# Pixel loads issued by ScalarE, a head norm in smaller operations, and five shared-expert blocks inside the attention's tail

## What is computed

```python
h = patches(x) @ W.T + b                       # 768 pixels a patch
# differential attention, 16 heads of 2 x 8, causal, 49 tokens
q, k, v = split(layernorm(h) @ w_attn)
att = softmax(mask(q @ k.T / 8))               # two maps a head
out = (att[0] - lam * att[1]) @ v
out = out * rsqrt(mean(out**2, 16 numbers) + 1e-5) * gamma * 0.8
h = h + out @ w_proj
# mixture of experts: 16 experts of 128, top 2, and a shared one of 512
xt = layernorm(h)
w, inds = top2(softmax(xt @ Wg.T)); w = w / sum(w)
y = sum_k w[k] * We_down[inds[k]] @ (silu(We_gate[..] @ xt) * (We_up[..] @ xt))
s = (silu(xt @ Ws_gate.T) * (xt @ Ws_up.T)) @ Ws_down.T
h = h + y + sigmoid(xt @ Wsg.T) * s
```

## Time and profile before

| | us |
|---|---|
| median of 3 runs (lowest, highest) | 452.35 (452.29, 455.34) |
| profiled execution | 452.69 |
| its span | 450.8 |
| PE busy | 365.3 (81%) |
| POOL busy | 274.9 (61%) |
| DVE busy | 262.5 (58%) |
| ACT busy | 205.9 (46%) |

### The profile page before, as it was taken

One profiled execution on the slowest core, in us unless ns is written; L12 is line 12 of the kernel. 1 busy time (PEld: TensorE's weight loads), 2 busy tenths in 40 slices (PEclk: granted clock), 3 DMA queues, 4 the chain that ended last, 5 costly groups with the idle time before them and its releaser, 6 DMA issues.

```text
span 450.8 us, 10482 instructions
## 1 busy us (share of the span) xinstructions
PE 365.3 (81%) x3418; PEld 329.9 (73%) x3419; DVE 262.5 (58%) x662; ACT 205.9 (46%) x512; POOL 274.9 (61%) x384
## 2 busy tenths in 40 slices
...
GB/s 271 105 69 68 94 94 117 62 63 107 93 86 91 114 104 78 85 114 86 126 112 1 1 1 1 0 399 239 69 71 74 120 125 135 129 127 103 22 203 225
DMA packets 33344, 47.17 MB, mean 105 GB/s; under 512 B 4538, under 2 KB 26750, under 8 KB 32528
## 3 DMA queue, kind: packets, MB, share of 16 engines
...
...
## 4 chain that ended last, share of the span: by engine, by line
POOL 36%; PE 31%; issue 19%; DVE 8%; DMA 3%; SPq 2%; POOLq 1%; ACT 0%; DVEq 0%
PE bank L1067 16%; POOL rr L549 10%; PE pair L1067 5%; POOL on L526 4%; POOL x_l L495 4%; PE bank L1295 3%; POOL att L534 3%; POOL parts L508 3%; POOL sq L542 2%; PE bank L1259 2%; POOL wsh_l L592 2%; POOL hn2T_l L565 2%; POOL rs L503 2%; DMA xr<-xt 2%; DVE h L1057 2%
## 5 line engine op out<-in xcount | busy, mean ns | idle before, releaser
L1157 PE MATMUL pair<-vx,PT 113*113 113x128 f32 x512 | 69.5, 279 | 1.6 <-issue 1.6
L900 DVE TENSOR_REDUCE smax<-bank 128x8 f32<-128x392 f32 x64 | 36.1, 564 | 48.9 <-PE bank L1136 48.7
L1157 PEld LDWEIGHTS pair<-vx,PT 113*113 113x113 f32 x512 | 61.6, 180 | 2.8 <-issue 1.8
L631 POOL DMA_INDIRECT picked<-by,bid x40 | 39.5, 988 | 28.0 <-DVE by L1046 18.2
L723 ACT ACTIVATE PT<-bank 113x456 f32<-113x456 f32 x64 | 35.3, 552 | 41.1 <-PE bank L1146 40.1
L1146 PE MATMUL bank<-cs,Sm 114*113 114x114 f32 x256 | 41.9, 286 | 11.5 <-DVE Sm L908 11.5
L549 POOL TENSOR_TENSOR rr<-ms,half_neg 128x16 f32<-128x16 f32 x16 | 46.7, 2916 | 1.3
L1079 PE MATMUL bank<-wt_h,x_h 128*98 128x256 f32 x96 | 31.9, 333 | 17.8 <-POOL x_l L495 11.2
L611 POOL DMA_INDIRECT slots_x<-hn2x,slot_u x32 | 34.9, 1092 | 18.4 <-issue 9.1
L526 POOL TENSOR_TENSOR on<-raw,rz 128x256 f32<-128x256 f32 x32 | 20.1, 629 | 42.2 <-DVE rz L943 42.2
L495 POOL TENSOR_TENSOR x_l<-xr,x_h 128x588 fp32r<-128x588 f32 x16 | 24.9, 1556 | 31.5 <-ACT x_h L643 31.5
...
## 6 DMA issues: line engine op xcount, KB each, us to landing
...
```

Source lines behind the costliest of these rows:

```text
L631: G.indirect_dma_start(out=picked, out_offset=bass.IndirectOffsetOnAxis(ap=bid[q][:], axis=0), in_=by[q][:], in_offset=None, bounds_check= ...
L900: V.tensor_reduce(smax[u % 2][:], score_of(u), AX.X, ALU.max).then_inc(maxed, 1)
L1157: last = T.matmul(bank[4 + b][0:JT, m * 2 * VN:(m + 1) * 2 * VN].rearrange("p (j n) -> p j n", j=2), PT[b][:, m, 0:JT], vx[i % NVX][:, :, ...
```

## The change

It has these parts. SP issues only pixel loads 0 and 1; ACT issues the other 14, each in front of the split of the tile before it, once POOL has split the tile that last used the buffer. SP's stack copies follow each other without loads between them. The bias is loaded third and has a semaphore of its own, so that the first embedding doesn't wait for the small loads. In the embedding steps DVE makes `rest` before it normalises. The head norm becomes: DVE ms2, ACT Ln and Exp (a first inverse root r0), and four 128x16 operations on POOL (one Newton step, with the factor in the projection's weights changed to match). The exponentials of the routing weights go from ACT to POOL as powers of e, and what DVE makes of them stands behind the offsets. Shared-expert blocks 0 to 4 have all their products in slots 66 to 79 and their Silu, multiply and splits in slots 70 to 81 and in the routing; the multiplies of blocks 4 and 5 and their splits stand between routing operations. Expert weight splits begin with block 7, one a block.

```diff
-            for i in range(2, 10):
-                load_x(i)
-            for d in range(4 * PARTS):
-                if d % 4 == 0:
-                    load_x(10 + d // 4)
-                stack(0, d)
-            for g in range(1, NGRP):
+            for g in range(NGRP):
...
             def head_norm(t):
-                pool.wait_ge(ms_done, t + 1)
-                G.tensor_tensor(ms2[:], ms[:], eps_sq[:], ALU.add).then_inc(ms2_done, 1)
-                pool.wait_ge(ms2_done, t + 1)
+
+                pool.wait_ge(r0_done, t + 1)
+                G.tensor_tensor(nt1[:], r0[:], r0[:], ALU.mult).then_inc(newton, 1)
+                pool.wait_ge(newton, 4 * t + 1)
+                G.tensor_tensor(nt2[:], nt1[:], ms2[:], ALU.mult).then_inc(newton, 1)
+                pool.wait_ge(newton, 4 * t + 2)
+                G.tensor_tensor(nt3[:], three[:], nt2[:], ALU.subtract).then_inc(newton, 1)
+                pool.wait_ge(newton, 4 * t + 3)
                 need(pool, ao_done, t)
-                G.tensor_tensor(rr[:], ms2[:], half_neg[:], ALU.pow).then_inc(rr_done, 1)
-                pool.wait_ge(rr_done, t + 1)
+                G.tensor_tensor(rr[:], r0[:], nt3[:], ALU.mult).then_inc(newton, 1)
+                pool.wait_ge(newton, 4 * t + 4)
                 need(pool, ao_turned, t)
...
+            pool.wait_ge(gate_diff, 1)
+            pool.wait_ge(logit_done, NT)
+            G.tensor_tensor(ed[:], euler[:], dl[:], ALU.pow).then_inc(e_exp, 1)
+            G.tensor_tensor(ez[:], inverse_euler[:], logits[:, :, E], ALU.pow).then_inc(e_exp, 1)
...
+            def load_x(i):
+                act.wait_ge(x_lo, i - 1)
+                act.wait_ge(x_hi, i - 1)
+                act.dma_start(xr[i % 2][:].rearrange("p k t -> p (k t)"), xt[i * 128:(i + 1) * 128, :]).then_inc(x_in[i % 2], 16)
...
+                if i + 2 < NT:
+                    load_x(i + 2)
...
+            def shared_silu(v):
+                act.wait_ge(sh_g, v + 1)
+                need(act, sh_h, v)
+                A.activation(sgl[:], bank[2 * v % 4][:, 0:SH], ACT.Silu).then_inc(sh_silu, 1)
+
+            def shared_high(v):
+
+                act.wait_ge(sh_h, v + 1)
+                need(act, sh_y, 4 * (v // SB - 1))
+                A.activation(hs_h[v // SB % 2][:, v % SB, :], hs[:], ACT.Copy).then_inc(sh_hi, 1)
+
+            SILU_AT = {70: 0, 72: 1, 73: 2, 76: 3, 81: 4}
+            HIGH_AT = {72: 0, 73: 1, 75: 2, 77: 3}
...
+                if (t := tile_at(u, 9)) is not None:
+                    act.wait_ge(ms2_done, t + 1)
+                    A.activation(lnr[:], ms2[:], ACT.Ln).then_inc(ln_done, 1)
+                    act.wait_ge(ln_done, t + 1)
+                    need(act, newton, 4 * t)
+                    A.activation(r0[:], lnr[:], ACT.Exp, scale=-0.5).then_inc(r0_done, 1)
...
+                if u in HIGH_AT:
+                    shared_high(HIGH_AT[u])
+                if u in SILU_AT:
+                    shared_silu(SILU_AT[u])
...
-            act.wait_ge(gate_diff, 1)
-            A.activation(ed[:], dl[:], ACT.Exp).then_inc(e_exp, 1)
-            A.activation(ez[:], logits[:, :, E], ACT.Exp, scale=-1.0).then_inc(e_exp, 1)
...
+            for v in range(DRAINED - 1, NU):
+                if v >= DRAINED:
+                    shared_silu(v)
+                shared_high(v)
+                if 0 <= v - FIRST_SPLIT < NG:
+                    split_expert(v - FIRST_SPLIT)
...
-                if 0 <= i - 1 < NT:
-                    norm(i - 1)
                 if i - 1 in QK_STEP:
                     n = QK_STEP[i - 1]
                     qk_rest(n, bank[n % 2])
+                if 0 <= i - 1 < NT:
+                    norm(i - 1)
...
+            def shared_hidden(v):
+                dve.wait_ge(sh_silu, v + 1)
+                dve.wait_ge(sh_u, v + 1)
+                need(dve, sh_hi, v)
+                need(dve, sh_lo, v)
+                V.tensor_tensor(hs[:], sgl[:], bank[(2 * v + 1) % 4][:, 0:SH], ALU.mult).then_inc(sh_h, 1)
+
+            def shared_low(v):
+                dve.wait_ge(sh_hi, v + 1)
+                need(dve, sh_y, 4 * (v // SB - 1))
+                V.tensor_tensor(hs_l[v // SB % 2][:, v % SB, :], hs[:], hs_h[v // SB % 2][:, v % SB, :].bitcast(F32), ALU.subtract).then_inc(sh_lo, 1)
+
+            HIDDEN_AT = {71: 0, 73: 1, 74: 2, 76: 3}
+            LOW_AT = {72: 0, 74: 1, 75: 2, 77: 3}
...
+                    dve.wait_ge(ms_done, t + 1)
+                    need(dve, newton, 4 * t - 2)
+                    V.tensor_scalar(ms2[:], ms[:], 1.0 / 16.0, EPS, ALU.mult, ALU.add).then_inc(ms2_done, 1)
+                if u in LOW_AT:
+                    shared_low(LOW_AT[u])
+                if u in HIDDEN_AT:
+                    shared_hidden(HIDDEN_AT[u])
...
-            dve.wait_ge(e_exp, 2)
-            link(V.tensor_scalar(ed1[:], ed[:], 1.0, None, ALU.add))
-            link(V.reciprocal(w1[:], ed1[:]))
-            V.tensor_tensor(w2[:], w1[:], ed[:], ALU.mult).then_inc(weights_known, 1)
-            link(V.tensor_scalar(ez1[:], ez[:], 1.0, None, ALU.add))
-            V.reciprocal(sig[:], ez1[:]).then_inc(weights_known, 1)
+            shared_hidden(DRAINED - 1)
...
+            shared_low(DRAINED - 1)
...
+            shared_hidden(DRAINED)
...
+            shared_low(DRAINED)
...
+            dve.wait_ge(e_exp, 2)
+            link(V.tensor_scalar(ed1[:], ed[:], 1.0, None, ALU.add))
+            link(V.reciprocal(w1[:], ed1[:]))
+            V.tensor_tensor(w2[:], w1[:], ed[:], ALU.mult).then_inc(weights_known, 1)
+            link(V.tensor_scalar(ez1[:], ez[:], 1.0, None, ALU.add))
+            V.reciprocal(sig[:], ez1[:]).then_inc(weights_known, 1)
+
+            shared_hidden(DRAINED + 1)
+            shared_low(DRAINED + 1)
...
+            for v in range(DRAINED, NU + DOWN_LAG):
+                if DRAINED + 2 <= v < NU:
+                    shared_hidden(v)
+                    shared_low(v)
+                if 0 <= v - FIRST_SPLIT < NG:
+                    split_expert(v - FIRST_SPLIT)
+                shared_down(v - DOWN_LAG)
...
-            SHARED_AT = {66: (0, 0), 67: (0, 1), 69: (1, 0), 70: (1, 1)}
+            SHARED_AT = {66: (0, 0), 67: (0, 1), 69: (1, 0), 70: (1, 1), 71: (2, 0), 72: (2, 1), 73: (3, 0), 75: (3, 1), 76: (4, 0), 79: (4, 1)}
...
+            for v in range(DRAINED, NU + DOWN_LAG):
+                if v < NU:
+                    shared_product(v, 0)
+                    shared_product(v, 1)
+                shared_down(v - DOWN_LAG)
```

More of the change, by code:

```diff
@@ L1 @@
+import math
 from contextlib import ExitStack
@@ L138, in build @@
         up_bf = keep("up_bf", [128, 128], BF16)
+        euler = keep("euler", [TT, NT])
+        inverse_euler = keep("inverse_euler", [TT, NT])
         shared = Zone(kept.at, ceiling)
@@ L185, in build @@
         pad = ea("pad", [128, ROW])
-        half_neg = ea("half_neg", [128, 2 * HP])
-        eps_sq = ea("eps_sq", [128, 2 * HP])
+        half_neg = ea("half_neg", [128, 1])
+        three = ea("three", [128, 2 * HP])
         eps_1 = ea("eps_1", [128, 1])
@@ L213, in build @@
         ms2 = ea("ms2", [128, 2 * HP])
+        lnr = ea("lnr", [128, 2 * HP])
+        r0 = ea("r0", [128, 2 * HP])
+        nt1 = ea("nt1", [128, 2 * HP])
+        nt2 = ea("nt2", [128, 2 * HP])
+        nt3 = ea("nt3", [128, 2 * HP])
         rr = ea("rr", [128, 2 * HP])
@@ L222, in build @@
         la = late.take
-        we_h = la("we_h", [128, EGU], F32R)
-        we_raw = Zone(late.at, ceiling).take("we_raw", [128, EGU])
-        we_l = la("we_l", [128, EGU], F32R)
         sgl = la("sgl", [128, SH])
@@ L229, in build @@
         hs_l = [la(f"hs_l{n}", [128, SB, SH], F32R) for n in range(2)]
+        we_h = la("we_h", [128, EGU], F32R)
+        we_raw = Zone(late.at, ceiling).take("we_raw", [128, EGU])
+        we_l = la("we_l", [128, EGU], F32R)
         ma = Zone(late.at, ceiling).take
```

65 lines of the change are left out of this document (18 added, 47 removed).

## The result

| | before | after |
|---|---|---|
| median, us | 453.85 (4 runs) | 423.54 (4 runs, 421.49 to 423.98) |
| profiled execution | 452.69 | 423.27 |
| its span | 450.8 | 421.4 |

The account below looks back on a forecast made before the run. Bounds: pixel loads queued between slow copies, PE's wait for Sm in the attention, PE after routing. 452.69 - 11.5 - 5 + 1.5 - 3.8 = 433.9 us profiled, median 433.5, range 425 to 443.

Parts of the forecast that it names:

- Behind slot_u (-3.8): Shared expert and scatter after slot_u: the scatter becomes the bound, blocks start 5.8 us earlier, PE's lower clock costs 2; bounds -6 and 0.
- Head norm in the attention (-5): Attention: only periods where POOL is late gain, 6.3 us less about 1 for ACT's extra waits; bounds +3 and -10.
- Embedding (-11.5): Start to first scores: copies become the bound but begin earlier, scores at 79.0 instead of 90.55; bounds -7 and -18.
- the marks of 75 and 84: Embedding's end: the prediction is wrong if first scores come before 75 or after 84 us.
- x_h of tiles 11 to 15 waiting under 2 us: Embedding, a sign to look for: these tiles no longer wait over 2 us for pixels.
- the scores need all 24 copies at 1.52 us: End of embedding: first scores wait for the first group's 24 stack copies, 37.8 us from the first issue.
- The rival of copies that run faster alone: Embedding: if copies beat 1.52 us each, PE's 15 + 3 us count, giving 427 us; chance 0.12.
- The rival that loads are no faster on ACT: Embedding: loads compete with copies for engines, only start and reordering gain (-4.2), giving 441 us; chance 0.12.
- Tail (+1.5): Tail and routing: shorter head norms give -3.5, added shared-expert work in the instruction order outweighs it; bounds -2 and +6.
- the sum: Whole kernel: profiled 452.69 us with the four terms applied, 433.9 us profiled.

## Why the prediction was wrong in size

1. **Behind slot_u (-3.8)**: right. From the end of slot_u the first block load comes after 49.1 us (48.8) and the first block after 51.3 (51.2), the rest is 1.9 longer (2), -3.8 in all. PE is idle for 5.1, not 3, and of the 1.9 only 0.6 came back when the wait was covered.
2. **Head norm in the attention (-5): the step that failed.** I wrote that this gives only what POOL is late, and took PE's waits, 11.5 us, as the ceiling. Between the fifth and the last smax the gain is 10.1. What I had priced came out near its price: 3.6 in the three periods with a pad transfer (2.7), 3.5 in slots 52, 56 and 60, the last two with a weight split (3.6), and 1.6 off (1) in slots 55, 59 and 63, where PE waits 0.5 us for ACT, which has waited for ms2 before (slot 59):

```profile
224.96 0.22 ACT L762 ACTIVATE lnr<-ms 128x16 f32<-128x16 f32 x1 [1.20 <-DVE ms L993]
...
228.47 1.10 PE L1211 MATMUL pair<-vx,PT 113*113 113x128 f32 x8 [0.51 <-ACT raw L743]
```

Two sums I had at nothing. One is 3.0 in slots 45 and 61, where PE's matmuls ran at 0.50. The profile of before had shown this: the mean clock of that stretch was 0.96 of 181 us, 7 us below full. The other is 1.5 in slots 23 to 25, where `on` follows rz by 0.3 us. Its cause is open: PE waits 1.6 us before `pair` there, for nothing that the trace names, and the kernel with the pad transfers on ACT gained the same 1.5 with the old head norm. Another 0.6 came before the fifth smax, where the clock was low from 90 to 97 us.
3. **Embedding (-11.5)**: two errors that partly cancel, so the first scores stayed inside the marks of 75 and 84 that I had set, and the attention had no such mark. Of the condition for it, x_h of tiles 11 to 15 waiting under 2 us, only tile 11 came true: four tiles wait 2.7 to 3.9. And the step "the scores need all 24 copies at 1.52 us" failed: 1.15 us each, no wait of PE. First copy and start were nearly right (42.05 for 41.2, so 3.4 of 4.2 us). The rival of copies that run faster alone had the right effect for the wrong reason: with no load they take 1.6 us, beside or just behind a load on the other queue mostly 0.8 to 1.2. Its price of -6.5 assumed that no pixels are waited for; 2.6 came of it.
4. **The rival that loads are no faster on ACT** fell: the embedding's edits alone bring 13 us, 3.2 of them by an earlier first copy. The Trainium skill, "DMA: Bandwidth & Descriptors", section "Issuing engines are not separate DMA queues", says that starting transfers on several engines saves only the sequencer's time. The trace disagrees here: with the same 14 loads of 294 KB on ACT's queue SP's copies took 1.15 us each and the waits for pixels 12.3 us (20.0 before), and the loads no longer stood behind copies whose operands weren't ready.
5. **Tail (+1.5)**: -0.8. Newton gave 4.6 to 4.9, where I had 3.5; the shared blocks cost 3.3 to 4.1, where I had 5.0. The mechanisms were those named, and hn2x of tile 15 follows its statistics by 2.3 us. ScalarE's table load took 1.28 us and Silu started right behind it, as before the change; the 2.66 us of the Trainium skill's page "ScalarE: Activation LUTs", section "What ACT_TABLE_LOAD costs", didn't show.

Of the 10.6 us that the profiled executions lie apart from the sum, 5.7 are the attention's, 2.6 the embedding's, 2.3 the tail's.
